# Attention layer of a language-model tower on one core: where the layer-norm statistics of a half are made, and how the row maxima are grouped

## The reference, cut to what matters

```python
h = W.T[tokens]                                  # 8 x 1024 x 256
xh = layernorm(h).reshape(b, c, 16, 16).transpose(0, 2, 1, 3)
q, k, v = split(xh @ Wqkv + bqkv, 3)             # 16 heads of width 16
att = softmax(tril(q @ k.T / 4, k=-1))           # masked scores are 0, not -inf
h = h + (att @ v).transpose(...).reshape(b, c, d) @ Wr + br
```

## Time and profile before

| what | us |
|---|---|
| median of 3 runs | 2999.05 (2997.51 to 3005.18) |
| the profiled execution's own time | 3005.22 |
| its span, first to last instruction | 3002.8 |
| PE busy in the span | 2581.3 (86%) |
| DVE busy in the span | 2118.6 (71%) |
| mean granted clock of PE | 0.928 |

### The profile page before, as it was taken

One profiled execution on the slowest core, in us unless ns is written; L12 is line 12 of the kernel. 1 busy time (PEld: TensorE's weight loads), 2 busy tenths in 40 slices (PEclk: granted clock), 3 DMA queues, 4 the chain that ended last, 5 costly groups with the idle time before them and its releaser, 6 DMA issues. The chain is left out here.

```text
span 3002.8 us, 58475 instructions
## 1 busy us (share of the span) xinstructions
PE 2581.3 (86%) x15254; PEld 1510.3 (50%) x15318; DVE 2118.6 (71%) x5668; ACT 1523.5 (51%) x3246; POOL 1640.4 (55%) x2564
## 2 busy tenths in 40 slices
PE   1778988888988888888868999898998979999999
PEld 0323433333333333343345666666666647666666
DVE  2657766777766767676567999898888965556554
ACT  1345555555555655555513655555555634444444
POOL 3664343333334333334245877777776757777675
PEclk7679999999999999999969999999999979999999
DMA  3353343344343344334230000000000000000000
GB/s 56 89 116 62 52 63 54 52 70 69 51 63 56 53 59 70 58 54 63 36 137 1 1 1 1 1 1 1 1 1 1 1 3 16 16 14 16 16 16 18
DMA packets 81300, 113.27 MB, mean 38 GB/s; under 512 B 25100, under 2 KB 37144, under 8 KB 80536
## 3 DMA queue, kind: packets, MB, share of 16 engines
q1 hardware_dynamic: 76360, 101.44, 19.8%
q0 software_dynamic: 3072, 8.39, 1.0%
q10 hardware_dynamic: 1744, 2.16, 0.2%
HBM read 18.98 MB, written 8.39 MB: 9 GB/s over the span
## 5 line engine op out<-in xcount | busy, mean ns | idle before, releaser
L554 ACT ACTIVATE probs<-scoresT 128x512 f32<-128x512 f32 x1152 | 639.7, 604 | 632.4 <-PE scoresT L697 622.9
L643 DVE TENSOR_REDUCE cand<-ring 128x4 f32<-128x512 f32 x1152 | 724.1, 680 | 219.6 <-PE ring L753 167.3
L476 POOL TENSOR_SCALAR_AFFINE_SELECT probs<-probs 128x256 f32<-128x256 f32 x512 | 204.9, 414 | 468.5 <-ACT probs L554 462.4
L697 PE MATMUL scoresT<-stage 98*128 98x512 bf16 (+3 forms) x1536 | 410.3, 344 | 22.2 <-ACT probs L554 16.6
L753 PE MATMUL ring<-Km,Qm 64*128 64x512 bf16 (+2 forms) x1792 | 253.0, 321 | 160.5 <-DVE cand L643 130.5
L717 PE MATMUL pv<-probs,Vg 128*32 128x512 f32 (+3 forms) x3072 | 325.2, 545 | 28.3 <-POOL probs L476 25.9
L753 PEld LDWEIGHTS ring<-Km,Qm 64*128 64x128 bf16 x1792 | 83.5, 95 | 375.6 <-DVE cand L643 239.5
L1180 PE MATMUL mm<-w_W,hT 128*128 128x256 f32 x1024 | 259.1, 399 | 8.7 <-ACT z L1268 2.8
L1200 PE MATMUL mm<-w_W,x2T 128*128 128x512 f32 x512 | 242.4, 596 | 0.3 <-DVE x L1419 0.2
L697 PEld LDWEIGHTS scoresT<-stage 98*128 98x128 bf16 x1536 | 114.5, 99 | 234.4 <-issue 139.1
L1261 ACT ACTIVATE hT<-mmT,w_be,w_g 128x128 f32<-128x128 f32 x512 | 185.5, 469 | 90.7 <-PE mmT L1191 90.7
(11 more groups left out here) (254 smaller groups left out, 5280.9 us busy)
## 6 DMA issues: line engine op xcount, KB each, us to landing
stage<-parts SPq DMA_DIRECT2D x256, 96.0 KB, 2.8
stage<-parts SPq DMA_DIRECT2D x256, 64.0 KB, 2.8
Qm<-parts SPq DMA_DIRECT2D x128, 128.0 KB, 2.6
Km<-parts SPq DMA_DIRECT2D x128, 128.0 KB, 2.7
stage<-parts SPq DMA_DIRECT2D x256, 32.0 KB, 2.4
out<-result SPq DMA_DIRECT2D x64, 128.0 KB, 1.7
stage<-ct SPq DMA_DIRECT2D x128, 4.0 KB
w_W<-in_W SPq DMA_DIRECT2D x4, 512.0 KB
```

The lines of the kernel that those rows point to most:

```text
L476: nc.gpsimd.affine_select(out=d, in_=d, compare_op=ALU.is_gt, fill=0.0, base=0, pattern=[[0, 2], [1, P]], channel_multiplier=-1).then_inc( ...
L554: nc.scalar.activation(probs[:, buffer(slot), :], scoresT[slot % SCORE_BANKS][:], ACT.Exp, scale=SOFT).then_inc(exp_ok, 1)
L643: ins = nc.vector.tensor_reduce(c, src[:].rearrange("p (t a b) -> p t a b", t=c.shape[1], b=P), AX.X, ALU.max)
L697: ins = nc.tensor.matmul(scoresT[slot % SCORE_BANKS][:, at:at + hi - lo], Ks[0:ROWS, gi, hh, P * kt:P * kt + P], Qs[0:ROWS, gi, hh, lo:hi] ...
```

## The change

The statistics of a half (now in four parts of two tiles, positions 20, 23, 25 and 28) and the power on POOL (a step of its own, LN_POWER, at position 28) move from the even pass into the odd pass of the half two ahead of its use, so a half's `mv` and `rstd` exist when its even pass begins. The start ("init") makes the statistics of halves 0 and 1, the second at position 13. The last half but one gets a section of its own ("late"), because no statistics follow it. Normalizing is cut into four parts at positions 1, 2, 4 and 5, the two transposes XT move to 4 and 7. The maxima come at nine positions of each pass, two MX steps (four banks) at each. Smaller moves: RSUM from 5 to 3, QK from (11, 13, 18, 20) to (9, 13, 17, 20), the four WR steps from positions 1, 1, 2, 2 to 2, 4, 6, 8, bursts 0 to 3 from (9, 12, 20, 28) to (11, 15, 22, 30), the copy PV_HALF from 14 to 17.

```diff
-BURST_AT = {0: 9, 1: 12, 2: 20, 3: 28}
+BURST_AT = {0: 11, 1: 15, 2: 22, 3: 30}
+MAX_AT = (0, 3, 7, 11, 15, 18, 22, 26, 30)
+LN_LATER = 13
 AT = {
-    0: {"LN_STATS": 1, "LN_NORM": 3, "XT": 7, "PV_COPY": 4, "EQ": 6, "TMP": 0, "PT": 5, "OT": 24, "WR": 25, "RSUM": 5, "SUF": 12, "QK": (11, 13, 18, 20), "MID_LAG": 2, "V": 21, "VG": 5, "LOAD": 0, "MX": 2, "MX_END": 32, "MX_CURVE": 1.0, "PV_HALF": 14},
-    1: {"PV_COPY": 4, "EQ": 6, "TMP": 0, "PT": 5, "WR": 1, "V": 8, "VG": 6, "LOAD": 0, "MX": 1, "MX_END": 32, "MX_CURVE": 1.0, "PV_HALF": 14},
+    0: {"LN_NORM": (1, 2, 4, 5), "XT": (4, 7), "PV_COPY": 4, "EQ": 6, "TMP": 0, "PT": 5, "OT": 24, "WR": 25, "RSUM": 3, "SUF": 12, "QK": (9, 13, 17, 20), "MID_LAG": 2, "V": 21, "VG": 5, "LOAD": 0, "PV_HALF": 17},
+    1: {"LN_STATS": (20, 23, 25, 28), "PV_COPY": 4, "EQ": 6, "TMP": 0, "PT": 5, "WR": 2, "V": 8, "VG": 6, "LOAD": 0, "PV_HALF": 17},
...
+    for ahead in stats:
+        for n in range(LN_PARTS):
+            at(pos_of["LN_STATS"][n] + (0 if scores else LN_LATER * (ahead - 1)), ("LN_STATS", ahead, n))
+        at(pos_of["LN_STATS"][-1] + (0 if scores else LN_LATER * (ahead - 1)), ("LN_POWER", ahead))
...
-            at(pos_of["WR"] + (j // 2 if scores else 0), ("R", "WR", "dve", j))
+            at(pos_of["WR"] + (2 * j if scores else 0), ("R", "WR", "dve", j))
...
-        lo, hi = pos_of["MX"], pos_of["MX_END"]
         for n, u in enumerate(uses):
-            at(int(lo + (hi - lo) * (n / len(uses)) ** pos_of["MX_CURVE"]), *u)
+            at(MAX_AT[n // 2] if scores else pos_of["MX"] + n, *u)
...
-            with eng.Fori(1, HALVES - 1) as hb:
+            with eng.Fori(1, HALVES - 2) as hb:
                 run("loop", hb, hb - 1)
+            run("late", HALVES - 2, 0)
             run("last", HALVES - 1, 0)
...
-                        elif kind == "LN_NORM":
-                            wait_apart(pool, (mv_ok, hb + 2))
+                        elif kind == "LN_POWER":
+                            hn = hb + e[2]
+                            wait_apart(pool, (mv_ok, LN_PARTS * (hn + 1)))
...
                         if kind == "LN_STATS":
+                            hn, part = hb + e[2], range(LN_TILES * e[3], LN_TILES * e[3] + LN_TILES)
                             if section == "init":
                                 dve.wait_ge(gat0, 16 * TPB)
-                            elif section == "loop":
+                            elif section == "first":
                                 dve.wait_ge(gat1, 16 * (TILES - TPB))
-                            for t in range(TPB):
+                            for t in part:
                                 ins = nc.vector.bn_stats(st[:, t, :], h[:, TPB * (hn // 2) + t, :])
                             ins.then_inc(stats_c, 1)
-                            wait_apart(dve, (stats_c, hn + 1))
+                            used = [] if e[2] == 1 or e[3] else [(xn_ok, TPB * hn)]
+                            wait_apart(dve, (stats_c, LN_PARTS * hn + e[3] + 1), *used)
...
                         elif kind == "LN_NORM":
                             dve.wait_ge(rstd_ok, hn + 1)
-                            for t in range(TPB):
+                            for t in range(LN_TILES * e[2], LN_TILES * e[2] + LN_TILES):
```

More of the change, by code:

```diff
@@ L54 @@
 PROBS = 16
+LN_PARTS = 4
+LN_TILES = TPB // LN_PARTS
 def score_slots():
@@ L130, in wait_apart, with window @@
         eng.wait_ge(sem, value)
+LN_LATER = 13
 AT = {
-    0: {"LN_STATS": 1, "LN_NORM": 3, "XT": 7, "PV_COPY": 4, "EQ": 6, "TMP": 0, "PT": 5, "OT": 24, "WR": 25, "RSUM": 5, "SUF": 12, "QK": (11, 13, 18, 20), "MID_LAG": 2, "V": 21, "VG": 5, "LOAD": 0, "MX": 2, "MX_END": 32, "MX_CURVE": 1.0, "PV_HALF": 14},
-    1: {"PV_COPY": 4, "EQ": 6, "TMP": 0, "PT": 5, "WR": 1, "V": 8, "VG": 6, "LOAD": 0, "MX": 1, "MX_END": 32, "MX_CURVE": 1.0, "PV_HALF": 14},
+    0: {"LN_NORM": (1, 2, 4, 5), "XT": (4, 7), "PV_COPY": 4, "EQ": 6, "TMP": 0, "PT": 5, "OT": 24, "WR": 25, "RSUM": 3, "SUF": 12, "QK": (9, 13, 17, 20), "MID_LAG": 2, "V": 21, "VG": 5, "LOAD": 0, "PV_HALF": 17},
+    1: {"LN_STATS": (20, 23, 25, 28), "PV_COPY": 4, "EQ": 6, "TMP": 0, "PT": 5, "WR": 2, "V": 8, "VG": 6, "LOAD": 0, "PV_HALF": 17},
     "V_IN": 0, "WR_IN": 1,
 }
-ALONE = {"LN_STATS": 0, "LN_NORM": 1, "XT": 2, "QK": (8, 9, 10, 11), "MID_LAG": 1, "V": 12, "PV_COPY": 1, "TMP": 2, "PT": 5, "OT": 11,
-         "WR": 14, "VG": 14, "LOAD": 14, "MX": 15, "MX_END": 35, "MX_CURVE": 1.0}
-def window(gi, ot, wr, tail, prologue, v, scores, following, load_max=False):
+ALONE = {"LN_STATS": (0, 0, 0, 0), "LN_NORM": (1, 1, 1, 1), "XT": (2, 2), "QK": (8, 9, 10, 11), "MID_LAG": 1, "V": 12, "PV_COPY": 1, "TMP": 2, "PT": 5, "OT": 11,
+         "WR": 14, "VG": 14, "LOAD": 14, "MX": 15}
+def window(gi, ot, wr, tail, prologue, v, scores, following, load_max=False, stats=()):
     others = {}
@@ L155, in window @@
     if prologue:
-        at(pos_of["LN_STATS"], ("LN_STATS",))
-        at(pos_of["LN_NORM"], ("LN_NORM",))
-        at(pos_of["XT"], ("R", "XT", "act", 0), ("R", "XT", "act", 1))
+        for n in range(LN_PARTS):
+            at(pos_of["LN_NORM"][n], ("LN_NORM", n))
+        for n in range(2):
+            at(pos_of["XT"][n], ("R", "XT", "act", n))
+    for ahead in stats:
+        for n in range(LN_PARTS):
+            at(pos_of["LN_STATS"][n] + (0 if scores else LN_LATER * (ahead - 1)), ("LN_STATS", ahead, n))
+        at(pos_of["LN_STATS"][-1] + (0 if scores else LN_LATER * (ahead - 1)), ("LN_POWER", ahead))
     if tail:
@@ L222, in plan @@
     v1, wr1 = bool(AT["V_IN"]), bool(AT["WR_IN"])
+    even = dict(ot=True, wr=not wr1, tail=True, prologue=True, v=not v1, scores=True, following=True, load_max=True)
+    odd = dict(ot=False, wr=wr1, tail=True, prologue=False, v=v1, scores=True, following=True, load_max=True)
+    none = dict(ot=False, wr=False, tail=False, prologue=False, v=False, scores=True, following=True, load_max=True)
     sections = {
[L224 to L228, removed]
+        "init": window(1, **(none | dict(prologue=True, v=True, scores=False, stats=(1, 2)))),
+        "first": window(0, **(none | dict(prologue=True, v=not v1))) + window(1, **(none | dict(tail=True, v=v1, stats=(2,)))),
+        "loop": window(0, **even) + window(1, **(odd | dict(stats=(2,)))),
+        "late": window(0, **even) + window(1, **odd),
+        "last": window(0, **(even | dict(prologue=False, v=False, load_max=False)))
+                + window(1, **(odd | dict(v=False, following=False, load_max=False))),
+        "final": window(0, **(none | dict(ot=True, wr=True, tail=True, scores=False, following=False, load_max=False))),
     }
     out, at = {}, (0, 0, 0)
-    for name in ("init", "first", "loop", "last", "final"):
-        out[name], end = number(sections[name], at)
+    for name, events in sections.items():
+        out[name], end = number(events, at)
         per = tuple(b - a for a, b in zip(at, end))
         out[name + "/per"] = per
-        at = tuple(a + (HALVES - 2) * p for a, p in zip(at, per)) if name == "loop" else end
+        at = tuple(a + (HALVES - 3) * p for a, p in zip(at, per)) if name == "loop" else end
     assert out["loop/per"][0] % RING_BANKS == 0
@@ L479, in run @@
                                 gather(TPB + gi * UNITS + slot, gat1)
-                        elif kind == "LN_NORM":
-                            wait_apart(pool, (mv_ok, hb + 2))
+                        elif kind == "LN_POWER":
+                            hn = hb + e[2]
+                            wait_apart(pool, (mv_ok, LN_PARTS * (hn + 1)))
                             nc.gpsimd.tensor_scalar(rstd[:], mv[:, :, 1], EPS, None, ALU.add).then_inc(rs_c, 1)
-                            pool.wait_ge(rs_c, hb + 2)
+                            pool.wait_ge(rs_c, hn + 1)
                             nc.gpsimd.tensor_tensor(rstd[:], rstd[:], minus_half[:], ALU.pow).then_inc(rstd_ok, 1)
```

## The result

| | before | changed |
|---|---|---|
| median of 4 runs each, us | 3000.76 | 2954.11 (2952.49 to 2954.40) |
| ratio, 95% interval | | 0.9842 (0.9825 to 0.9860) |
| span of the profiled execution | 3002.8 | 2952.5 |
| start to the last CT of the attention layer | 1485.0 | 1478.9 |
| expert stage (first `in_ps` to first `gate` matmul) | 851.2 | 805.9 |

The kernel became faster by 47 us (1.6%), near the 59 that were forecast and inside the range. The table shows that this is not the forecast come true. The attention layer, the only part the change edits, gained 6.1 us up to its last CT. The stage of the experts, whose code is the same line for line, gained 45.3. The rest of the program became longer, by 0.5 us between the two and by 0.6 behind them. Together this is the span's 50.3. A pass is measured here from the transpose CT at the end of the pass before to its own.

What follows compares the result with a forecast made beforehand. PE sets the pace, held mainly by DVE's reading of the ring. Fifteen even passes at 4.3 us give 64.5, less 6 once is 58.5; the profiled 3005.22 becomes 2946.7, the median 2940, range 2895 to 2982.

Steps and rivals of the forecast that it cites:

- The even pass: Attention layer's even passes: maxima alternating with normalizing, without the wait for POOL's power, gain 4.3 us in each of fifteen.
- The bound of 2.14 for eight: DVE's normalizing: eight took 2.14 us at the start with POOL idle; the forecast used the loop's 3.77.
- Rival A: Even passes: the stall is only cut up and the clock still falls; 35 us won, 2964 us, chance 0.22.
- The odd pass: Attention layer's odd passes: 3.35 us of added DVE statistics are hidden by PE's own work; cost taken as 0.
- The end I gave for the loss, 3.35: Odd pass, worst case: all 3.35 us of the added DVE statistics fall on the path.
- The ring waits of four-bank groups are small: Attention passes: PE's waits for maxima read four banks at a time are small with three or more slots between groups.
- rival D: Attention passes: four-bank groups make PE wait 0.4 us at each of 18 per half; slower, 3051 us, chance 0.06.
- The power on POOL: End of the odd pass: the power, about 2.0 us with the addition, is covered by 3.5 of POOL idle; cost 0.
- rival C: POOL's power is late at position 28, so burst 4 waits 2.0 us in 14 odd passes; 2995 us, chance 0.06.
- Once only: First odd pass: its statistics now wait for the last gather, delaying DVE and PE by 6 us (0 to 8).
- The start: Start of the layer: the second set of statistics falls into 27.71 us of DVE waiting for loads; cost 0.
- The section of its own costs code, not work: 0: Attention layer's last half but one: its separate section adds code but no work; cost 0.

Runs made afterwards that it cites:

- run 4: The changed kernel with the odd pass's statistics cut from 8 bn_stats and 8 bn_aggr to 4 bn_aggr; mean odd pass 41.01 us, even 45.94.
- run 12: The kernel of run 9 with the odd pass's statistics cut to 4 bn_aggr; mean odd pass 37.44 us, even 46.47.
- Run 5: The kernel before with only the maxima grouped by four banks at nine positions in both passes; 3148.12 us against 3003.51 for the kernel before.
- run 3: The changed kernel with the odd pass's maxima spread again at their old positions; 2957.19 us, ratio 0.9823.
- run 6: The changed kernel with bursts back at 9, 12, 20 and 28 and PV_HALF at 14 in both passes; odd pass 39.67 us, even 49.03.
- run 7: The changed kernel with the odd pass's four WR steps back at positions 1, 1, 2, 2; odd pass 42.05 us, even 46.89.
- run 9: The changed kernel with the odd pass's maxima, WR, bursts and PV_HALF as before, statistics still at 20, 23, 25, 28; 2937.93 us, ratio 0.9748.
- Run 8: The changed kernel with statistics at 8, 12, 16, 19 and the power at 19, except in the first odd pass; 2942.57 us.
- run 1: The kernel before with 148 one-column DVE memsets added in a stretch where DVE waits; 2967.04 us, ratio 0.9852 to the kernel before.
- run 2: The changed kernel with 108 one-column DVE memsets added in a stretch where DVE waits; 3003.64 us, ratio 0.9975 to the kernel before.
- run 10: The kernel of run 9 with the statistics at 8, 12, 16, 19 and the power at 19; 2944.56 us, ratio 0.9774.

## Why the prediction was right in its number and wrong in its reasons

**The even pass: right.** Forecast 4.3 us won, measured 5.0. The wait at the first XT was given as 1.6 and is 1.52. The second, given as 1.4, is 0.19: the third and fourth part of the normalizing took 1.10 us for four tiles, where I counted 1.9, beside an idle POOL. The bound of 2.14 for eight, from the start of the layer, was the better price for that half. Burst 0, with which the counted set of steps ends, is over at 663.98 (1.71 us from 662.27), 17.3 us into the pass, where the sum gave 18.2 and the kernel before 22.5. The rest of the pass is 29.1 us in both kernels, as forecast. Pass length forecast 46 to 48, measured 46.8. Rival A's sign, a clock of 0.5 some 10 us into the pass, is not there; the slow stretch at the start of the pass follows the waits at the end of the odd one.

**The odd pass: the step that failed in the sum.** "I take 0, between them, as both sides are hidden by PE's own work." It costs 4.5 us, thirteen times in halves 1 to 13, +58 us against the 70.5 that the fourteen even passes win. I compared sums of busy time over the pass, 30.8 for DVE against 33.7 for PE, and the sums did not show the waits of two engines that take turns on four banks, nor the clock that fell with them. The end I gave for the loss, 3.35, was too small as well, since it held only the statistics: the arrangement is 3.6 by itself (runs 4 and 12).

**"The ring waits of four-bank groups are small": wrong,** the second part of the same step. Run 5 shows 3.2 us in an odd pass and 6.6 in an even one from grouping alone. This is the mechanism of rival D, which I held for 0.06 since it would make the whole slower. Its sign, ring waits on DVE of over 8.6 us in a pair of passes, did not appear: those in the list come to 86.4 us in 1200, 6.3 a pair. It was also not the groups alone: runs 3, 6 and 7 each undo one part, and the odd pass answers with +0.4, -1.6 and +0.7. Undone together in the odd pass (run 9) they give 1.6, no more than the bursts alone gave in run 6. The old bursts in the odd pass only were not run, so whether run 9's gain is theirs alone is open.

**The power on POOL: hidden only in part.** I took 0 and gave rival C up to 2.0. Rival C's sign did not appear, as burst 4 waits only 0.29 for POOL. But CT, a step before it, waits 1.64 for POOL, once per odd pass. POOL and DVE in order of time, the changed kernel, at the end of that odd pass:

```profile
642.96 1.68 POOL L500 TENSOR_TENSOR rstd<-rstd,minus_half 128x8 f32<-128x8 f32 x1
644.60 0.78 POOL L491 TENSOR_SCALAR_AFFINE_SELECT probs<-probs 128x256 f32<-128x256 f32 x2
645.32 0.20 POOL L528 CAST c<-m 128x16 bf16<-128x16 f32 x1
```

```profile
642.39 2.45 DVE L661 TENSOR_REDUCE cand<-ring 128x4 f32<-128x512 f32 x4
644.88 0.30 DVE L651 TENSOR_REDUCE m<-cand 128x16 f32<-128x144 f32 x1
```

The power and the masks behind it end at about 645.3, when DVE's maximum is there too (645.18); the last four banks were read only from 642.39 on, behind the fourth part of the statistics. So the wait belongs to the late reduction on DVE at least as much as to POOL. Run 8, with the power at 19, still has about 1.0, as the even pass has.

**Once only: about right.** The first odd pass grew from 45.0 to 53.1 us, +8, where 6 was given; DVE's row there, from its timeline:

```profile
192.91 0.75 DVE L628 BATCH_NORM_STATS2 st<-h 128x6 f32<-128x256 f32 x2 [7.62 <-DMA h<-in_WT,tok]
```

It waits 7.62 us for the last gather. Between chips this pass alone differs by some 6 us (50.9 in run 1, where it is arranged as before). In the one set of runs that has both arrangements profiled, runs 1 and 2, it grew by 3.4 (50.9 to 54.3). The 6 lies between, and neither number is sharp.

**The start: right.** The second set of statistics is hidden, 95.3 and 95.5 us to the end of the first section.

**"The section of its own costs code, not work: 0": the step that hid the result.** It, and the other added code, gave 45.3 us. The sum by my own steps with the measured sizes is 70.5 + 3.1 + 0.6 in even passes, less 58.4, 8.1 and 1.3 in odd ones, or about 6 us. That the forecast of 2940 met 2954 was luck: an effect that I did not name was about as large as the loss that I missed. The rows for that effect were there: two groups of DVE waits for issue, eleven each, in the expert stage, and 92 instruction packets on the page. I read waits only in the stage that the change edits. A small slip beside it: the range ends at 2982, short of the 2984 that it was said to take in.

My own tests said so. Three of those that I wrote for "right" hold: no wait of 5.75 us, `xn` with no wait for POOL, an even pass of 46 to 48. But "the odd one 37 to 39" and "the forecast is wrong if the odd exceeds 40" turned against it, and from them alone the layer's gain would have been seen to vanish.

What stays open: which of the moved steps costs the idle time of the changed odd pass, beyond what runs 3, 6 and 7 show one at a time, and why the clock falls in runs 3, 4 and 10 although PE idles less there.

## What to carry to other kernels

Before pricing a change that adds or removes code, look for an engine that waits for issue at the first instruction of a hardware loop, in every stage: if it does, its time hangs on how many instructions stand ahead of it, and a gain or loss there belongs to no idea in the diff. Test it with padding in a covered stretch, and compare versions stage by stage, not by the whole. When two engines share a short ring of buffers, price a move by the order of the turns: work that fits by its sum can still stand between a full ring and its first read. And read idle time and clock beside each pass length: a run that takes waits away can have the same length at a lower clock.

## What the runs showed of the hardware that was not expected

- The expert stage, built on one hardware loop, took 806 to 810, 825 or 851 to 855 us for the same instructions, with waits of 0, 26 and 50 us on DVE at the loop's first instructions and 38 to 43, 97 and 92 to 98 instruction packets on one queue in the whole run. A shift of 148 instructions removed the wait from one kernel, one of 108 brought it to the other.
- Normalizing a tile of 128 columns on DVE took 0.27 us a tile with POOL idle (1.10 for four at 657.43) and 0.41 on average for the four at 653.47, beside POOL's copy and sums.
- The granted clock of an odd pass fell from 0.96 to 0.92 with no single PE wait over 1.64 us in it; a burst at 630.88 took 3.22 us, at a granted clock of 0.59, after waits of 0.41 and 1.16.
- With the maxima of the odd pass spread (run 3) PE idled 1.6 us less per odd pass than in the changed kernel and was busy 2.0 us longer with the same work, at 0.892 in place of 0.926.
